# Two transformer layers on one core: the order in which their steps alternate is written anew

## The reference, cut to what matters

```python
x = x + tanh(g_xattn[0]) * L0_xattn(layernorm(x), ctx, causal, padding)   # 32 heads of 8, 8 kv groups
x = x + tanh(g_ffn[0])   * L0_ffn(layernorm(x))    # Hadamard, 8-bit rows, ternary weights, relu^2
x = x + tanh(g_xattn[1]) * L1_xattn(layernorm(x), ctx)   # self and cross attention, fp8-rounded
x = x + tanh(g_ffn[1])   * L1_ffn(layernorm(x))    # 8 experts, the best 2 of each row
```

## Time and profile before

| | us |
|---|---|
| runs | 1433.47, 1430.90, 1432.77 |
| median | 1432.77 |
| the profiled execution | 1431.25 |
| its span, first to last instruction | 1429.2 |

### The profile page before, as it was taken

One profiled execution on the slowest core, in us unless ns is written; L12 is line 12 of the kernel. 1 busy time (PEld: TensorE's weight loads), 2 busy tenths in 40 slices (PEclk: granted clock), 3 DMA queues, 4 the chain that ended last, 5 costly groups with the idle time before them and its releaser, 6 DMA issues. The chain is left out here.

```text
span 1429.2 us, 29957 instructions
## 1 busy us (share of the span) xinstructions
PE 1286.4 (90%) x8831; PEld 949.3 (66%) x8847; DVE 1042.2 (73%) x2336; ACT 919.3 (64%) x3577; POOL 756.5 (53%) x1068
## 2 busy tenths in 40 slices
PE   3899999999988999999999999999999983369991
PEld 2344444444446888888888888888888863359991
DVE  6466666666686888888888888888888777835554
ACT  1345454545577988888888888888888843323330
POOL 2455555545455555666666666666555533823331
PEclk8799999999998999999999999999999995579996
DMA  6443333332132011110111001110120006322225
GB/s 143 104 78 54 72 54 72 54 70 53 40 111 82 2 38 37 37 37 0 37 37 37 21 16 37 37 37 1 38 72 1 1 1 211 122 77 81 83 75 176
DMA packets 134339, 83.50 MB, mean 58 GB/s; under 512 B 67309, under 2 KB 129774, under 8 KB 134256
## 3 DMA queue, kind: packets, MB, share of 16 engines
q1 hardware_dynamic: 125280, 72.50, 20.0%
q0 software_dynamic: 3744, 8.43, 1.6%
q10 hardware_dynamic: 5232, 1.54, 0.5%
HBM read 50.01 MB, written 34.00 MB: 59 GB/s over the span
## 5 line engine op out<-in xcount | busy, mean ns | idle before, releaser
L1422 POOL TENSOR_TENSOR head_rstd<-head_rstd,minus_half 128x4 f32<-128x4 f32 x192 | 239.0, 1245 | 15.1
L1410 ACT ACTIVATE squares<-ps 128x128 bf16<-128x128 f32 x768 | 201.2, 281 | 49.8 <-PE ps L1378 39.8
L1378 PE MATMUL ps<-l_wb,xq 128*128 128x512 f16 (+1 forms) x1024 | 209.9, 328 | 1.2 <-ACT headsT L1446 1.2
L1502 POOL TENSOR_TENSOR prob<-prob,rinv 128x512 f32<-128x512 f32 x128 | 135.2, 1056 | 115.7 <-DVE rinv L1497 114.2
L1489 ACT ACTIVATE prob<-ps,nmax 128x128 f32<-128x128 f32 x512 | 182.4, 383 | 11.8 <-DVE nmax L1480 11.7
L1446 ACT ACTIVATE headsT<-ps,l_hln 128x256 f32<-128x256 f32 (+1 forms) x256 | 166.0, 675 | 29.5 <-PE ps L1437 29.5
L1410 ACT ACTIVATION_READ_ACCUMULATOR squares<-ps 128x1 f32 x768 | 163.0, 212 | 0.0
L1430 DVE TENSOR_TENSOR heads_n<-ps,head_rstd 128x512 f32<-128x512 f32 x192 | 131.4, 684 | 27.9 <-POOL head_rstd L1422 27.8
L702 DVE TENSOR_REDUCE nmax<-ps 128x4 f32<-128x512 f32 x128 | 84.9, 683 | 72.7 <-PE ps L695 72.5
L1473 PE MATMUL ps<-headsT 128*128 128x128 f32 x1024 | 135.1, 275 | 0.0
L1378 PEld LDWEIGHTS ps<-l_wb,xq 128*128 (+1 forms) x1024 | 100.8, 98 | 47.4 <-issue 2.5
(11 more groups left out here) (303 smaller groups left out, 2763.9 us busy)
## 6 DMA issues: line engine op xcount, KB each, us to landing
slots<-blank_slot SPq DMA_DIRECT2D x16, 1161.0 KB, 5.7
taken<-slots SPq DMA_DIRECT2D x23, 258.0 KB
w_out_raw<-in_wprojT SPq DMA_DIRECT2D x8, 512.0 KB, 3.9
raw<-in_winT SPq DMA_DIRECT2D x4, 1024.0 KB, 8.0
raw<-in_woutT SPq DMA_DIRECT2D x4, 1024.0 KB, 5.7
back<-picked SPq DMA_DIRECT2D x8, 512.0 KB, 8.8
q_stack<-q_parts SPq DMA_DIRECT2D x48, 64.0 KB
k_blocks<-k_parts SPq DMA_DIRECT2D x192, 16.0 KB
```

The lines of the kernel that those rows point to most:

```text
L1378: last = e.matmul(out, xq[:, k, which, slot_at], weights(k, hl, c0, n), start=(k == 0 and hl == 0), stop=(k == KD - 1 and hl == 1))
L1410: last = e.activation(squares[:, 4 * n + h, :], A[n][:, h * HD1:(h + 1) * HD1], ACT.Square, scale=HD1**-0.5, accum_out=hss[:, 4 * n + h:4 ...
L1422: e.tensor_tensor(hr[:, four], hr[:, four], t["half"][:, four], ALU.pow).then_inc(g_r[n].sem, 1)
L1502: e.tensor_tensor(prob[:, kind, :, :], prob[:, kind, :, :], spread(rinv[:, kind, :], P), ALU.mult).then_inc(g_p[kind].sem, 1)
```

## The change

Only the five strings of `MIXED` change. The lists a, b and c are the same, and so are all instructions; each engine runs the same ones in another order across the junction.

```diff
     "tensor": (
         "aaaaaaaaaaaaaaaaaaaaaaaaaaaaaaaaaaaaaaaaaaaaaaaaaaaaaaaaaaaaaaaaaaaaaaaaaaaaaaaaaaaaaaaaaaaaaaaaaaaa"
-        "aaaaaaaaaaaaaaaaaaaaaaaaaaaaaaaaaaaaaaaaaaaaaaaabaaaaaaaaabaaaaaaababaabbaababbabbaabbbaabbbabbbbbbb"
-        "bbbbbbbbbbbbbbbbbbbbbbbbbbbbbbbbbbbbb"
+        "aaaaaaaaaaaaaaaaaaaaaaaaaaabaaaabaaaaaaaaaaaaaaaaaaaaaaaabaabaabbaabbaaababbaabbbaaabbbbbabbbaababbb"
+        "aabbbbbbbbbbbbbbbbbbbbbbbbbbbbbbbbbbb"
     ),
     "vector": (
-        "aaaaaaaaaaaaaaaaaaaaaaaaaaaaaaaaaaaaaaaaaaaaaaaaaaaaaaaaaaaaaaaabbaababaababcaabcbbbbaaacababbabbccb"
-        "abbbabbbbbbabcbbbbbbbbbbbbbbbbbbbbbbbbbbbbbbbbbbbbbbbbbbbbbbbbbbbcbbcb"
+        "aaaaaaaaaaaaaaaaaaaaaaaaaaaaaaaaaaaaaaaaaaaaaaaaaaabaabaaaaaaabbaaabababbabaabaabaccaabbbbbaaaabbabba"
+        "bbbbcbbbbabbabbbbbacbbcbbbbbbbbbbbbbbbbbbbbbbbbbbbbbbbbbbbbbbbbbcbbcbc"
     ),
     "scalar": (
-        "aaaaaaaaaaaaaaaaaaaaaaaaaaaaaaaaaaaaaaaaaaaaaaaaaaaaaaaaaaaaaaaaaaaacacaaabaabbbabbababaabacbabbabbb"
-        "ccabababbabbbbbabcbbbbbbbbbbbbbbbbbbbbbbbbbbbbbbcc"
+        "aaaaaaaaaaaaaaaaaaaaaaaaaaaaaaaaaaaaaaaaaaaaaaaaaaaaaaaaaaabbbaaaaabaaabbabcaaaababacababbabbaababba"
+        "bbabcbbbababbabbbabbbcabbcbbbbbbbbbbbbbbbbbbbbbccc"
     ),
-    "gpsimd": "aaaaaaaaaaaaaaaaaaaaaaaaaaaaaaaaaaaaaaaaaaaababaabbaaabbaabbaabbabbbbbbbbbbbbbbbbbbbbbbbbbbbbb",
-    "sync": "aaaaaaaabcccbbccccc",
+    "gpsimd": "aaaaaaaaaaaaaaaaaaaaaaaaaaaaaaaaaaaaababaaabaaabbbbaaabbaabbbaabbbabbbbbbbbbbbbbbbbbbbbbbbbbbb",
+    "sync": "aaaaaaabaccbbcccccc",
 }
```

## The result

| | before | after |
|---|---|---|
| runs | 15 | 15 |
| median, us | 1431.04 | 1434.33 |
| lowest to highest, us | 1429.35 to 1433.47 | 1432.21 to 1436.03 |
| span of the profiled execution, us | 1429.2 | 1432.5 |

The ratio is 1.0021, with a 95% interval of 1.0013 to 1.0029: the changed kernel is 1.9 to 4.1 us slower. The prediction was 1434.3.

What follows compares the result with a forecast made beforehand. PE was taken to bound the kernel, the junction the latency of layer 0's last feed-forward chain. -5 + 5.5 + 1.7 = +2.2 on 1431.25 gave 1433.5, plus 0.85 for the runs' mean 1434.3; range 1428.6 to 1440.

Steps and rivals of the forecast that it cites:

- The constants' stall: DVE's constants, now between `MX:2(15)` and `MX:3(15)`, leave PE idle before `S:5(15)`: 1.7 us, bounds 0 and 2.3.
- The idle time of the junction: Layer 1 begins sooner and fills gaps of batch 14's chain; PE's 12.5 us of idle become about 9: -3.5.
- rival C: Junction gives almost nothing, missed in-order waits on DVE from F2t(15) on, piece paid in full: +6.2, 1438.3; chance 0.37.
- The half clock in the junction: PE's loss at 1.2 GHz there falls from 5.3 to 3.7 us, the spell at 417 going: -1.6, bounds -5.3 and 0.
- rival B: Junction gives all it could, no spell at half clock: -8.8 there, -1.6 or -3.3 in sum, 1428.8; chance 0.10.
- sum of -5: Junction's idle and half-clock terms together: `*PV:1<0>` starts 5.1 us sooner, rounded to 5 us given back, between 1 and 9.
- The last weight piece: ACT waits for WP7's load behind its copy of WP5, so PE stands 6.7 us, before 1.2: +5.5, bounds +1.1 and +8.6.
- The clock behind the pause: PE runs at half clock after standing idle for 6.7 us: +1.7, bounds 0 to 3.
- SP and POOL at nothing: Reordered `*CL[b0]`, WP0, `*CL[b2]` and BL on SP and POOL cost 0; a load's time, 3.9 us, at most.
- Rival A: WP7's load is there in time, only one more ACT copy stays, +1.1: -3.9 in sum, 1428.2; chance 0.12.

Runs made afterwards that it cites:

- filled_pause: Changed kernel with 28 useless matmuls of 512 columns on PE just ahead of `*A:0<5>`, inside the pause: 1432.02 us, ratio 1.0004.
- early_piece: Changed kernel with weight pieces WP5 to WP7 brought forward, WP5 one round sooner on ACT and DVE: 1426.36 us, ratio 0.9967.
- extra_copy: Kernel of early_piece with one useless copy on ACT behind WP7, into a tile nobody reads: 1428.24 us, ratio 0.9979.
- late_piece: Kernel before, with only WP5 to WP7 moved to the changed kernel's places: 1438.64 us, ratio 1.0051.
- consts_split: Changed kernel with DVE's constants in two steps, the first links left in place, the other twelve instructions behind `NO:1(14)`: 1431.89 us, ratio 1.0007.
- all_together: Changed kernel with WP5 a round sooner, WP6 before `*ST:1<4>`, constants split, DVE's WP1 behind `*N:0<0>`, `F7v(15)` ahead of `*N:0<2>`: 1424.93 us, ratio 0.9944.

## Why the prediction was right, and where its parts were off

The mechanism and both large terms were right; that the smaller ones cancelled, and that the base was high, was luck. Step by step:

- **The constants' stall**: 1.7 on record, 1.81 in the trace. The time moved by +1.9 (0.6 to 3.1) when it was made alone and by about -2.0 when it was taken away, the two traces by +0.7 and -2.7, as spells at half clock went or moved with it. The size was lucky in part: how long the constants take depends on what GpSimd does beside them, see below.
- **The idle time of the junction**: waits of 1.1, 0.9, 2.1, 0.5, 1.05, 0.8 and 1.6 on record stand in the trace as 0.80, 0.79, 1.96, 0.55, 0.95, 0.74 and 1.18. Stepping thus named every wait of over 0.3 us, and none that I had missed appeared, which was rival C's case. The releasers agree where the prediction named one; before F3(15) the profile itself says only "issue", but F6q(14)'s last instruction ends on DVE at 432.95, 0.1 us before. The positions were less exact: `*A:2<0>` 1.3 us and F2t(15) 1.4 us later than on record (412.9 and 428.1 in the old clock). The term of -3.5 was too large all the same: -2.5 was measured. The step that failed is the deduction of 2 us for the last matmul's own run, in going from my waits to the profile's idle time; one microsecond would have been right.
- **The half clock in the junction**: -1.6 on record, -2.3 measured by busy time. Its start was low, too: in the three spells of before (416.2 to 419.8, 430.2 to 437.0 and 446.9 to 450.6 us) PE was busy for 2.81, 5.90 and 3.54 us, so some 1.8 us of them were idle, not 3, and close to 6 us were lost, not 5.3. Of the two spells I left only one came in the changed kernel's trace, from 436.6 to about 442 us; the waits of 0.95, 0.74 and 1.18 us before `*PV:1<0>` brought none (the clock is at 0.98 from 442 to 454). In filled_pause, with the same order up to there and the same waits to some 0.1 us, both came. Which spells come is thus not settled by the waits that I named, and rival B's case of none at all did not occur. That the two errors were nearly equal and opposite, so that the sum of -5 stood against -4.8, was luck.
- **The last weight piece**: +5.5 on record, 6.71 - 1.21 = 5.50 in the trace and gone again when the piece is moved (early_piece); ACT's wait 4.4 against 4.44; the load 3.9 against 3.9. Here the ring of buffers, the two issue rows and one landing time gave the whole. (The 3.2 us that the prediction takes from the Trainium skill come from a fit that its section gives for DMAs issued by GpSimd. SP issued these loads, so the 3.9 us don't speak against it; the sum didn't use it.)
- **The clock behind the pause**: +1.7 on record, 2.3 measured (filled_pause). The term was mis-sized: I took it from the spell at 447 us, behind waits of 2.91 and 1.00; the row at the start of the experts, some 2.3, would have been the better neighbour, as it too lies behind one long wait.
- **SP and POOL at nothing**: no wait for the context, for `BL` or for WP0 appears; the loss is accounted for without them.

The chances need a word. A difference of +0.21%, with 0.13 to 0.29 as its interval, lies on the bound of 0.2% that I drew between no change and slower. The sum of the terms was +2.2 us and the measured change is +3.3 by the medians, +3.0 (1.9 to 4.1) by the ratio, so the terms are near its lower end; that the time itself came out at 1434.3 is owed to a base that was 1.1 us too high (1431.25 + 0.85 = 1432.1, where 15 runs gave 1431.04). Rival A failed exactly where its counter-argument said: the wait lies in the order. With the piece moved, its case comes true: extra_copy, with the load there in time and the one more copy kept, measured 1428.24, and A said 1428.2, though from the base that was 1.1 us too high.

## What to carry to other kernels

When steps of several engines are re-ordered, follow each buffer of a ring round once: who frees it, who issues the load, who waits for it. Where an in-order engine has three uses of a ring of two in a row, it waits for a whole round inside its own list (its own copy, the other reader, the issue and the landing; here 4.4 us of ACT's time), whatever is free elsewhere. Here one letter moved in each of two strings gave back 8 us, more than the whole re-ordering had brought. Price the parts of such a change one by one: this one was a gain of 5 and a loss of 8, and its median alone would have said that nothing much had happened. And follow a forecast of the half clock with more than one trace: the same order brought different spells in different executions.

## What the runs showed of the hardware that I had not expected

**Short instructions of DVE held by GpSimd.** I priced the constants at 5.6 us, and they took 5.8, but not by the same instructions. DVE's rows of after, under them POOL's of the same stretch, and last one of DVE's rows of before:

```profile
379.15 0.80 DVE L1186 TENSOR_SCALAR l_row_w<-l_inv_insc,l_lnw 128x4 f32<-128x4 f32 x1
...
380.00 0.22 DVE L1186 TENSOR_SCALAR l_row_w<-l_inv_insc,l_lnw 128x4 f32<-128x4 f32 x1
...
380.84 0.73 DVE L1190 COPY l_head_eps<-l_wsc 128x4 f32<-128x4 f32 x1
381.61 0.65 DVE L1191 COPY l_head_eps<-l_wsc 128x4 f32<-128x4 f32 x1
...
383.11 0.23 DVE L1195 RECIPROCAL l_head_eps<-l_head_eps 128x12 f32<-128x12 f32 x1
```

```profile
378.04 1.90 POOL L1031 TENSOR_TENSOR unit_raw<-unit_raw,l_wscale 128x1024 f32<-128x1024 f32 x1
380.83 0.72 POOL L931 TENSOR_TENSOR fly<-hid 128x256 f32<-128x256 f32 x1 [0.90 <-ACT hid L926]
381.51 0.72 POOL L932 TENSOR_TENSOR fly<-hid 128x256 f32<-128x256 f32 x1
...
383.01 0.72 POOL L935 TENSOR_TENSOR hid<-fly 128x256 f32<-128x256 f32 x1
```

```profile
398.10 0.17 DVE L1190 COPY l_head_eps<-l_wsc 128x4 f32<-128x4 f32 x1
```

The copy L1190, of 4 elements in each row, takes 0.73 us when it starts 0.01 us after a GpSimd operation and took 0.17 before, when none ran. Each of the long ones ends with the GpSimd operation beside it: 379.95 and 379.94, 381.57 and 381.55, 382.26 and 382.23. The RECIPROCAL at 383.11 lies inside one as well and still takes its 0.23. The Trainium skill, page "SBUF — State Buffer", section "SBUF: two separate sides", says that VectorE and GpSimd share a pair of ports as an exclusive lock, held by whoever comes first for its whole instruction, and that among VectorE's operations those in a two-port mode want it, and those with two SBUF inputs when the GpSimd operation reads SBUF. The trace agrees in that the held ones end with GpSimd's operation and the RECIPROCAL isn't held; which of them ran in a two-port mode it doesn't show. Five of the nineteen small instructions were held so, for some 2.1 us together (their durations less those of their like), about as much as PE's stall of 1.81. In the trace of before it was four others (L1197, L1198, L1200 and L1201, 0.58 to 0.65 us each), held for some 1.9 us; so the 5.6 us on record already had such a hold in them, and that after had one of about the same size was luck. That the stall would be near nothing beside an idle GpSimd is an inference; no run tried it.

**The start of the span varies.** The same instructions ahead of the junction ran up to 3.5 us later in one profiled execution than in another, with the order there unchanged (an L806 at 337.65 us before, 341.16 in late_piece). It is why one trace's span cannot carry a difference of 2 us.

**The half clock does not follow from the waits alone.** From 388 to 436 us the PE waits of over 0.3 us are the same in after and filled_pause (0.80, 0.79, 1.96 and 0.55 or 0.66 us), and so are those before `*PV:1<0>` (0.95, 0.74, 1.18, to 0.01 us). In after the clock was at half from 436.6 to 442 and at 0.98 from 442 to 454; in filled_pause at 0.55 from 435.8 to 439.3 and at 0.57 from 452.7 to 456.2. In consts_split and all_together the waits of 1.96 and 0.65 us (0.66 in the latter) brought no spell (1.00 from 433.1 to 448.4 in the former), those before `*PV:1<0>` did. The total moves less: in the five traces with the changed junction and whole constants, `*O` of round 0 comes at 461.4 to 461.95 us in the old clock. What decides between the spells stays open.

**Useless matmuls in a pause pay.** 28 of them (6.21 us), in a wait that was there anyway, kept PE's clock at 1.00 through it and behind it (482.4 to 493.2 us) and gave 2.3 us. PE came to L1378 0.2 us later than without them by the traces; no engine shows a new wait.
